# Merging the last two value batches of each head pair in a two-layer transformer kernel

## The chip, the cores and the metric

The kernel runs on one core of a Trainium2 chip. Times are microseconds of device time for one launch. The time before is the median of three runs, 3097.34 us (3094.24 to 3098.24).

## The reference

Eight sequences of 512 tokens with 256 channels pass through two layers. Only the first layer's attention is touched. It has 16 heads and three attentions that share the queries; their outputs are mixed by a gate for each sequence:

```python
a1 = _attn(q, k1, v1, causal=True)    # keys and values from a latent of 32
a2 = _attn(q, ks, vs, causal=False)   # 64 selected tokens only
a3 = _attn(q, kw, vw, causal=True)    # keys and values of their own
g = gate[:, :, None, None, None]
out = g[:, 0] * a1 + g[:, 1] * a2 + g[:, 2] * a3
```

with `_attn` = softmax(q k^T / sqrt(96)) v, values 32 wide. Behind it come the output projection, a feed-forward part, and the second layer (causal attention with rotary positions, 16 heads of 16, and a product with signs).

## The kernel before

The work is cut into passes, one per layer and sequence, in the order (layer, sequence) = (0,0), (0,1), (1,0), (0,2), (1,1), ... (0,7), (1,6), (1,7). "Pass 5" below is layer 0 of sequence 5. A layer-0 pass runs over 8 pairs of heads, 0 to 7.

**Units.** For each pair the transposed scores are made in 12 units, each one psum bank of up to 128 keys by 512 queries: units 0 and 1 are A1's keys 0 to 127 for the two heads, 2 and 3 A1's key blocks 1 and 3, 4 and 5 A3's block 0, 6 and 7 A3's blocks 1 and 3, 8 and 9 block 2 of both A1 and A3 (256 queries each), 10 and 11 A2's 64 selected keys. `unit` (L1162 to L1164) issues three matmuls for each part on TensorE. ScalarE takes the exponential of the bank into one of eight slots of PR (L1839), GpSimd clears what lies above the diagonal (L1954), not for units 10 and 11, which are not masked.

**Batches.** The products with the values are issued by `values` (L1198) in batches listed in PV; batch k holds units 2k and 2k+1. Each part gives two matmuls per head, one with the values and one with a block of ones (row sums), into four column groups of the array (`128*32`, for A2 `64*32`), all accumulated in one psum bank for each attention: OB[A1], OB[A3], OB[A2]. Batch 4 (units 8 and 9) completes A1 and A3, batch 5 (units 10 and 11) A2; COMPLETE says so. A batch ends by raising `pv_done`.

**Behind a batch.** When an attention is complete, ScalarE copies its bank times the gate (`outputs`, L1824) and raises `evacuated`; behind the copy of A2, SP gathers the row sums by DMA (L836), VectorE inverts them (L1454), SP parks and spreads the inverses, VectorE scales the outputs (L1461), GpSimd sums the three (L1970, L1972) and raises `summed`.

**Next operands.** While pair p runs its units, the keys and values of the next pair are made in "pieces" on TensorE: pieces 0 to 3 and 4 (L1066, L1070), the latent keys (L1073), the latent values (L1076), piece 6 for the selected rows (L1081), each followed by transposes (`piece_tr`, L1093). ScalarE copies the results (L1724), VectorE multiplies by the rotary tables (L1400), and subtracts to get the low halves of a high/low split (L1390, L1419). The results of pieces, transposes, units and the row maxima (`max`, L1128) share a ring of five psum banks, taken in the planned order: a step waits until the bank's use five steps back has been read.

**Order.** `attention_steps` gives each step a planned time and sorts by it; every engine runs its steps in that one order. A unit i of pair p stands at 12p + i, a batch at 12p + its last unit + o["pv"], which is 2.66 here, an output at 0.3 behind its batch, the gather at 0.35. So on TensorE the end of a pair looks like this:

```
... unit 10, piece 1, mt, unit 11, pieces 2 and 3, piece_tr 0,
BATCH 4,
unit 0 of the next pair, piece 4, piece_tr 1, unit 1 of the next pair, piece 6, piece_tr 3,
BATCH 5,
unit 2 of the next pair, ...
```

(which pieces stand there varies a little with the pair). In pair 7 there is no next pair. Between its batches stand, in passes 0 to 6, steps that prepare the next pass, above all 16 matmuls that select rows by a one-hot matrix (L1051), made by VectorE (L1590). Behind batch 5 of pair 7 layer 1's work begins: ScalarE copies stacked rows (L1724, PR from R), GpSimd prepares them (L2018, L2020), TensorE transposes them (L1283). In pass 7 nothing stands between the two batches of pair 7.

Of the kernel before, what the change touches and what calls it, by code (L numbers as in the profile page):

```python
# [43 lines left out]
A1, A3, A2 = 0, 1, 2  # L44
# [65 lines left out]
def diagonal(layer, i):  # L110

    return [col for a, _, _, col in UNITS[layer][i] if layer or a != A2]


CAUSAL = [[i for i in range(NU[layer]) if diagonal(layer, i)] for layer in range(2)]
MASK0 = [0, NPAIR * len(CAUSAL[0])]
PV = [(2 * k, 2 * k + 1) for k in range(6)]
NPV = len(PV)


# [10 lines left out]
def before_pass(layer, s):  # L131

    done = [z[0] for z in PASSES[:PASSES.index((layer, s))]]
    return [sum(per[z] for z in done) for per in
            ([NPAIR * n for n in NU], [NPAIR * len(c) for c in CAUSAL], PRODUCTS, OUTS)]


UNIT0, MASK0, PV0, OUT0 = ({z: before_pass(*z)[k] for z in PASSES} for k in range(4))

COMPLETE = {4: [A1, A3], 5: [A2]}  # L140

# [147 lines left out]
def attention_steps(layer, s):  # L291
# [26 lines left out]
    def output(t, what, a, last):  # L318
        at.extend([(t + 0.3, ("out", what, a)), (t + 0.35, ("gather", what))][0:1 + last])
        if last and what < JOBS[layer] - 1:  # L320
            late = "late_" if layer == 0 and what == JOBS[0] - 2 else ""
            t1 = t + 0.35 + o[late + "recip"]
            normalise((layer, s, what), t1, t1 + o[late + "scale"])
# [8 lines left out]
    for p in range(NPAIR):  # L332
        for i in range(0 if layer else n):
            at.append((n * p + i, ("unit", p, i)))
            if i in CAUSAL[layer]:
                at.append((n * p + i + 1.2, ("mask", p, i)))
        for k, units in enumerate(() if layer else PV):
            t = n * p + units[-1] + o["pv"]
            at.append((t, ("pv", p, k)))
            for a in COMPLETE.get(k, []):  # L340
                output(t, p, a, a == A2)
# [203 lines left out]
def build_program(nc, x, w_small, w_imp, w_q, w_nv, w_kw, w_sel, w_proj, g_q, g_kv,  # L545
# [4 lines left out]
    with ctx:  # L550
# [83 lines left out]
        def sem(name):  # L634
            return ctx.enter_context(nc.semaphore(name))
# [4 lines left out]
        pv_done = sem("pv_done")  # L640
# [13 lines left out]
        exp_masked = sem("exp_masked")  # L654
        evacuated = sem("evacuated")
# [90 lines left out]
        def unit_number(s, layer, p, i):  # L746
            if layer:
                return UNIT0[layer, s] + len(QUAD) * (p // 2) + QUAD.index((p % 2, i))
            return UNIT0[layer, s] + p * NU[layer] + i
# [30 lines left out]
        def products_of(j):  # L780
# [5 lines left out]
            p, i = divmod(j - UNIT0[layer, s], NU[layer])  # L786
            return PV0[layer, s] + p * NPV + [i in units for units in PV].index(True) + 1

# [129 lines left out]
        def _(pe):  # L918
# [250 lines left out]
            def values(s, p, k):  # L1169

                units = PV[k]
                if units[-1] in CAUSAL[0]:
                    pe.wait_ge(exp_masked, MASK0[0, s] + p * len(CAUSAL[0]) + CAUSAL[0].index(units[-1]) + 1)
                else:
                    pe.wait_ge(exp_ready, unit_number(s, 0, p, units[-1]) + 1)
                if p and k in (0, 2, 5):

                    pe.wait_ge(evacuated, OUT0[0, s] + 3 * (p - 1) + {0: A1, 2: A3, 5: A2}[k] + 1)  # L1180
                elif s and k == 0:
                    pe.wait_ge(evacuated, OUT0[0, s])
                parts = [(i, part) for i in units for part in UNITS[0][i]]

                parts.sort(key=lambda x: (x[1][0], x[1][2], x[1][1]))
                for n in range(0, len(parts), 2):
                    for side in range(2):
                        for i, (a, h, j, col) in parts[n:n + 2]:
                            rows = KEEP if a == A2 else P
                            if side:  # L1190
                                v = ONES[0:rows, :]
                            elif a == A2:
                                v = VS[:, p % 3, h * VD:(h + 1) * VD]
                            else:
                                v = VV[:, p % 3, j, a, h * VD:(h + 1) * VD]
                            row = 64 * side + 32 * h
                            slot = unit_number(s, 0, p, i) % NP
                            last = mm(OB[a][row:row + 32, j * P:T], v, PR[0:rows, slot, col:col + T - j * P],  # L1198
                                      start=(j == 0), stop=(j == 2 or a == A2), skip_group_check=True)
                last.then_inc(pv_done, 1)  # L1200
# [85 lines left out]
            def attention(layer, s):  # L1286
                for x in STEPS[layer, s]:
# [6 lines left out]
                    elif x[0] == "max":  # L1294
                        max_scores(s, layer, x[1], x[2])
                    elif x[0] == "mt":
                        transpose_maxima(s, layer, x[1])
                    elif x[0] == "unit":
                        unit(s, layer, x[1], x[2])
                    elif x[0] == "pv" and layer == 0:  # L1300
                        values(s, x[1], x[2])
                    elif x[0] == "pv":
                        values_of_heads(s, x[1], x[2])
                    elif x[0] == "pro_pe":
                        prologue(x[1], x[2])
                    elif x[0] in ("wo_early", "wo_last", "sign") or x[0] == "hT" and x[2] == 3:
                        tail(x)
                    elif x[0] == "proj_early":
                        project_early(x[1])
                    elif x[0] == "proj_last":  # L1310
                        project_last(x[1])
                    elif x[0] == "hT":
                        transpose_half(x[1], x[2], x[3])
                    elif x[0] == "fc":
                        hidden_units(*x[1:])
                    elif x[0] == "y":
                        second_products(*x[1:])
                    elif x[0] == "qk":
                        queries_and_keys(*x[1:])
                    elif x[0] == "v":  # L1320
                        values_of_half(*x[1:])
                    elif x[0] == "heads":
                        transpose_heads(*x[1:])
# [396 lines left out]
        def _(act):  # L1720
            a = nc.scalar

            def copy(dst, src):
                return a.activation(dst, src, ACT.Copy)  # L1724
# [89 lines left out]
            def outputs(s, layer, n, att):  # L1814

                if layer == 0:
                    act.wait_ge(pv_done, PV0[0, s] + n * NPV + (6 if att == A2 else 5))
                    if s + n:
                        act.wait_ge(summed, NPAIR * s + n)
                    if n == 0:  # L1820
                        act.wait_ge(gates_ready, s + 1)
                        act.wait_ge(scaled1, NG * max(s - 1, 0))
                    g = 1 if att == A1 else 2 if att == A3 else 0
                    a.activation(OE[:, att, :], OB[att][:, :], ACT.Copy, scale=GG[:, g:g + 1]).then_inc(evacuated, 1)  # L1824
                else:
                    act.wait_ge(pv_done, PV0[1, s] + (n + 1) * len(QUAD_PV))
                    if n == 0:
                        act.wait_ge(summed, NPAIR * min(s + 2, B))
                    if s and n < 3 or n >= 3:
                        act.wait_ge(scaled1, NG * s + max(n - 2, 0))  # L1830
                    copy(OE[:, n % 3, :], OB[n % 3][:, :]).then_inc(evacuated, 1)
# [280 lines left out]
```

## Time and profile before

| | |
|---|---|
| median of the runs | 3097.34 us |
| the profiled execution | 3094.82 us |
| its span | 3093.1 us |
| TensorE busy | 2884.6 us (93%) |
| VectorE busy | 1980.4 us (64%) |
| ScalarE busy | 1483.6 us (48%) |
| GpSimd busy | 958.1 us (31%) |
| matmuls at L1198 | 2304 with ones, 2048 with VV, 256 with VS |
| mean granted TensorE clock | 0.968 |

The span runs from the first to the last instruction of one profiled execution; 1.7 us of its own time lie outside. PE is TensorE, PEld its weight loads, DVE VectorE, ACT ScalarE, POOL GpSimd. Matmuls are pipelined and their ends are modelled, so the distances between the starts of matmuls are read rather than their durations. The granted clock is the share of full speed.

### The profile page before, as it was taken

The numbers are of one execution on the slowest core, as the hardware profiler recorded it, in microseconds if no ns is written. First come the engines' busy times: TensorE is split into PE (matmuls) and PEld (weight loads), VectorE is DVE, ScalarE is ACT, GpSimd is POOL, SyncE is SP. The second block draws the span as 40 slices with busy tenths as digits, with TensorE's granted clock in tenths as the row PEclk, the third lists the DMA queues.
The fourth block names the chain that finished last, engine by engine and source line by source line (L and its number), as shares of the span: only waits on it lengthen the run. The fifth ranks groups of instructions, "written<-read, shape, count | busy, mean of one in ns | idle before, by whom it ended". The sixth has DMA issues, their size and how long they took to land. (4 is left out here: it accounts for less than half of the span.)

```text
span 3093.1 us, 53525 instructions
## 1 busy us (share of the span) xinstructions
PE 2884.6 (93%) x18384; PEld 2056.4 (66%) x18384; DVE 1980.4 (64%) x6275; ACT 1483.6 (48%) x3132; POOL 958.1 (31%) x1700
## 2 busy tenths in 40 slices
PE   6999899989999899999999989998999989999877
PEld 5666676667766677666776667666676666766654
DVE  5666557675586656766666766677566676665644
ACT  2554344464445644455445554445544554445433
POOL 1233232432333313333233332233223332333231
PEclk8999999999999999999999999999999999999989
DMA  3111001001110010100111001110011000110000
GB/s 121 33 33 31 27 26 37 19 18 33 35 33 19 24 37 26 32 24 19 37 32 33 17 26 37 33 31 14 27 39 32 26 18 23 32 32 18 14 8 29
DMA packets 58700, 91.42 MB, mean 30 GB/s; under 512 B 19904, under 2 KB 32704, under 8 KB 58176
## 3 DMA queue, kind: packets, MB, share of 16 engines
q1 hardware_dynamic: 58432, 88.01, 9.6%
q8 instruction: 148, 2.42, 0.3%
q14 instruction: 120, 0.98, 0.1%
HBM read 81.68 MB, written 5.24 MB: 28 GB/s over the span
## 5 line engine op out<-in xcount | busy, mean ns | idle before, releaser
L1839 ACT ACTIVATE PR<-work 128x512 f32<-128x512 f32 (+1 forms) x1088 | 640.3, 598 | 715.6 <-PE work L1164 608.9
L1438 DVE CUSTOM_DVE_ANT_0 work<-work,KEEPB 128x128 f32<-128x128 f32 (+3 forms) x1536 | 665.8, 477 | 95.6 <-PE work L1128 94.1
L1954 POOL TENSOR_SCALAR_AFFINE_SELECT PR<-PR 128x256 f32<-128x256 f32 (+1 forms) x960 | 362.0, 381 | 872.7 <-ACT PR L1839 868.4
L1128 PE MATMUL work<-BIG 96*128 96x448 f32 (+8 forms) x1664 | 454.6, 364 | 31.8 <-DVE NMX L1438 17.4
L1162 PE MATMUL work<-BIG 99*128 99x512 f32 (+4 forms) x1152 | 420.0, 365 | 11.0 <-DVE BIG L1419 8.6
L1943 POOL TENSOR_TENSOR TOK<-AB 128x256 f32<-128x256 f32 (+1 forms) x320 | 216.6, 677 | 636.7 <-DVE AB L1400 601.6
L1198 PE MATMUL outs<-PR,ONES 128*32 128x512 f32 (+4 forms) x2304 | 407.7, 461 | 0.0
L1419 DVE TENSOR_TENSOR BIG<-work,BIG 96x512 fp32r<-96x512 f32 (+1 forms) x320 | 191.5, 604 | 324.3 <-ACT BIG L1724 324.0
L1128 PEld LDWEIGHTS work<-BIG 96*128 96x128 f32 (+1 forms) x1664 | 278.5, 199 | 157.6 <-issue 64.1
L1163 PE MATMUL work<-BIG 96*128 96x512 f32 (+4 forms) x1152 | 382.7, 332 | 0.0
L1164 PE MATMUL work<-BIG 96*128 96x512 f32 (+4 forms) x1152 | 380.6, 330 | 0.0
L1724 ACT ACTIVATE BIG<-work 96x512 fp32r<-96x512 f32 (+5 forms) x624 | 353.4, 569 | 40.0 <-PE work L1093 29.4
L1198 PE MATMUL outs<-PR,VV 128*32 128x512 f32 (+3 forms) x2048 | 337.7, 440 | 3.7 <-POOL PR L1954 3.7
L1724 ACT ACTIVATE TOK<-work 128x128 f32<-128x128 f32 (+1 forms) x320 | 85.5, 267 | 516.8 <-issue 229.3
L1162 PEld LDWEIGHTS work<-BIG 99*128 99x128 f32 (+1 forms) x1152 | 210.1, 182 | 167.1 <-issue 100.7
L1070 PE MATMUL work<-WKW,HT 128*128 128x256 f32 x1024 | 276.5, 394 | 0.0
L1400 DVE TENSOR_TENSOR AB<-work,ROPE 128x512 f32<-128x512 f32 (+1 forms) x320 | 201.0, 629 | 114.7 <-PE work L1070 91.0
L1441 DVE TENSOR_REDUCE NMX<-work 128x1 f32<-128x64 f32 (+1 forms) x640 | 170.4, 283 | 123.4 <-PE work L1128 119.6
L1164 PEld LDWEIGHTS work<-BIG 96*128 96x128 f32 (+1 forms) x1152 | 213.1, 185 | 23.8
L1163 PEld LDWEIGHTS work<-BIG 96*128 96x128 f32 (+1 forms) x1152 | 212.6, 185 | 8.3 <-issue 2.0
L1070 PEld LDWEIGHTS work<-WKW,HT 128*128 128x128 f32 x1024 | 196.0, 198 | 16.2
L1093 PE MATMUL work<-ID,TOK 128*96 128x128 f32 x1152 | 179.5, 275 | 18.3 <-ACT VV L1724 4.2
(178 smaller groups left out, 4620.1 us busy)
## 6 DMA issues: line engine op xcount, KB each, us to landing
NRM<-park SPq DMA_DIRECT2D x112, 192.0 KB, 3.1
WKW<-w_kw_dram SPq DMA_DIRECT2D x64, 256.0 KB, 2.7
WSEL<-w_sel_dram SPq DMA_DIRECT2D x64, 256.0 KB, 3.0
R<-park SPq DMA_DIRECT2D x72, 64.0 KB, 2.0
HN<-x_dram SPq DMA_DIRECT2D x8, 512.0 KB, 4.8
X<-x_dram SPq DMA_DIRECT2D x8, 512.0 KB, 3.9
out_dram<-X SPq DMA_DIRECT2D x7, 512.0 KB, 3.2
R<-park SPq DMA_DIRECT2D x16, 192.0 KB, 3.0
```

Source lines behind the costliest of these rows:

```text
L1070: last = mm(ps[:, 192:448], HT0[:, c, t * P:(t + 1) * P], WKW[:, g % 2, c, :], start=(c == 0), stop=(c == NC - 1))
L1128: last = mm(ps[:, col:col + n], q, k, start=(i_mm == 0), stop=(i_mm == len(u["mm"]) - 1))
L1162: mm(out, k[0][0:D0 + 3], q[0][0:D0 + 3], start=(col == 0), stop=False)
L1163: mm(out, k[0][0:D0], q[1][0:D0], start=False, stop=False)
L1164: last = mm(out, k[1][0:D0], q[0][0:D0], start=False, stop=stop)
L1198: last = mm(OB[a][row:row + 32, j * P:T], v, PR[0:rows, slot, col:col + T - j * P], start=(j == 0), stop=(j == 2 or a == A2), skip_group_c ...
L1400: read_work(v.tensor_tensor(rotations(i, rows, heads), src.unsqueeze(1).broadcast_to(shape), ROPE0[0:rows, t, :, :].unsqueeze(2).broadcast ...
L1438: last = v.tensor_tensor_reduce(ps[:, lo:hi], ps[:, lo:hi], KEEPB[:, T - (hi - lo):T], -1.0, -NEG, ALU.add, ALU.min, dst)
L1724: return a.activation(dst, src, ACT.Copy)
L1839: a.activation(PR[0:rows, j % NP, :], ps[0:rows, :], ACT.Exp).then_inc(exp_ready, 1)
L1943: gp.tensor_tensor(dst.rearrange("p h (j d) -> p h j d", j=2), a4, b4[:, :, ::-1, :], ALU.add).then_inc(tok_ready, 1)
L1954: gp.affine_select(blocks, blocks, [[0, len(cols)], [1, P]], ALU.is_ge, 0.0, base=0, channel_multiplier=-1).then_inc(exp_masked, 1)
```

## The change

PV gets five batches instead of six: the last holds units 8, 9, 10 and 11 and completes A1, A3 and A2. By the planning rule its time is 12p + 11 + 2.66, which is where batch 5 stood. Before it, TensorE waits for the mask of unit 9, the exponential of unit 11, and for the previous pair's A2 output to be copied (A1's and A3's were awaited by batches 0 and 2). The copies of A1 and A3 are planned at 0.3 behind the merged batch, ahead of A2's, and wait for the fifth `pv_done` of the pair. The matmuls themselves, and their order within a batch (A1, A3, A2), are the same.

```diff
-PV = [(2 * k, 2 * k + 1) for k in range(6)]
+PV = [(2 * k, 2 * k + 1) for k in range(4)] + [(8, 9, 10, 11)]
...
-COMPLETE = {4: [A1, A3], 5: [A2]}
+COMPLETE = {4: [A1, A3, A2]}
...
                 units = PV[k]
-                if units[-1] in CAUSAL[0]:
-                    pe.wait_ge(exp_masked, MASK0[0, s] + p * len(CAUSAL[0]) + CAUSAL[0].index(units[-1]) + 1)
-                else:
+                masked = [i for i in units if i in CAUSAL[0]][-1]
+                pe.wait_ge(exp_masked, MASK0[0, s] + p * len(CAUSAL[0]) + CAUSAL[0].index(masked) + 1)
+                if masked != units[-1]:
                     pe.wait_ge(exp_ready, unit_number(s, 0, p, units[-1]) + 1)
-                if p and k in (0, 2, 5):
+                if p and k in (0, 2, 4):
 
-                    pe.wait_ge(evacuated, OUT0[0, s] + 3 * (p - 1) + {0: A1, 2: A3, 5: A2}[k] + 1)
+                    pe.wait_ge(evacuated, OUT0[0, s] + 3 * (p - 1) + {0: A1, 2: A3, 4: A2}[k] + 1)
...
-                    act.wait_ge(pv_done, PV0[0, s] + n * NPV + (6 if att == A2 else 5))
+                    act.wait_ge(pv_done, PV0[0, s] + n * NPV + 5)
```

## Rows read from the trace of the kernel before

**Rows 1.** The page's first part: busy time, share of the span, instructions.

```profile
PE 2884.6 (93%) x18384; PEld 2056.4 (66%) x18384; DVE 1980.4 (64%) x6275; ACT 1483.6 (48%) x3132; POOL 958.1 (31%) x1700
```

**Rows 2.** Waits of TensorE: us in total, times, longest us.

```profile
PE work L1283 <- POOL PR L2020: 17.7, 15, 8.2
...
PE work L1081 <- DVE BIG L1419: 5.8, 18, 0.7
...
PE work L1066 <- DVE BIG L1390: 3.0, 8, 0.9
```

**Rows 3.** Timeline of TensorE, pass 5, pair 5 to 6: start, duration, [wait].

```profile
2059.59 0.60 PE L1093 MATMUL work<-ID,TOK 128*96 128x128 f32 x4
...
2061.12 0.50 PE L1162 MATMUL work<-BIG 99*128 99x512 f32 x1
...
2063.59 0.50 PE L1162 MATMUL work<-BIG 99*128 99x512 f32 x1
...
2064.86 1.13 PE L1081 MATMUL work<-WSEL,SELT 128*128 128x256 f32 x4 [0.29 <-DVE BIG L1419]
...
2066.36 0.62 PE L1198 MATMUL outs<-PR,VS 64*32 64x512 f32 x2
```

**Rows 4.** Timeline of TensorE, pass 4: transposes, then a unit, no batch between.

```profile
1552.60 0.60 PE L1093 MATMUL work<-ID,TOK 128*96 128x128 f32 x4
1552.95 0.48 PE L1162 MATMUL work<-BIG 99*128 99x512 f32 x1
```

**Rows 5.** Timeline of TensorE, end of pass 7: starts of batches 4 and 5.

```profile
2853.38 0.41 PE L1198 MATMUL outs<-PR,VV 128*32 128x256 f32 x2
...
2854.38 0.62 PE L1198 MATMUL outs<-PR,VS 64*32 64x512 f32 x2
```

**Rows 6.** Timeline of ScalarE in the stretch of rows 3.

```profile
2059.64 1.20 ACT L1724 ACTIVATE BIG<-work 32x512 fp32r<-32x512 f32 x2
2063.14 0.28 ACT L1724 ACTIVATE TOK<-work 128x128 f32<-128x128 f32 x1 [2.31 <-issue]
...
2063.90 1.26 ACT L1824 ACTIVATE NRM<-outs,GG 128x512 f32<-128x512 f32 x2
...
2068.31 0.68 ACT L1824 ACTIVATE NRM<-outs,GG 128x512 f32<-128x512 f32 x1
```

**Rows 7.** Timeline of VectorE in the stretch of rows 3.

```profile
2060.94 1.40 DVE L1390 TENSOR_TENSOR BIG<-work,BIG 32x512 fp32r<-32x512 f32 x2 [3.63 <-ACT BIG L1724]
2062.37 0.69 DVE L1400 TENSOR_TENSOR AB<-work,ROPE 128x512 f32<-128x512 f32 x1
2064.12 0.69 DVE L1419 TENSOR_TENSOR BIG<-work,BIG 96x512 fp32r<-96x512 f32 x1 [1.06 <-ACT BIG L1724]
```

**Rows 8.** Timelines of VectorE and TensorE, pass 5, pair 1 to 2.

```profile
1926.79 0.69 DVE L1419 TENSOR_TENSOR BIG<-work,BIG 96x512 fp32r<-96x512 f32 x1 [1.06 <-ACT BIG L1724]
...
1928.02 0.48 PE L1162 MATMUL work<-BIG 99*128 99x512 f32 x1
```

**Rows 9.** Timeline of VectorE, pass 3, behind pair 1's outputs.

```profile
1184.27 0.55 DVE L1454 RECIPROCAL NRM<-NRM 48x64 f32<-48x64 f32 x1 [0.26 <-DMA NRM<-NRM]
```

**Rows 10.** Timelines of TensorE, ScalarE and GpSimd, end of pass 5.

```profile
2112.61 0.62 PE L1198 MATMUL outs<-PR,VS 64*32 64x512 f32 x2
...
2114.14 0.69 ACT L1824 ACTIVATE NRM<-outs,GG 128x512 f32<-128x512 f32 x1 [0.22 <-PE outs L1198]
2114.85 1.15 ACT L1724 ACTIVATE PR<-R 128x512 fp32r<-128x512 f32 x2
...
2116.08 0.73 POOL L2018 TENSOR_TENSOR PR<-R,PR 128x256 fp32r<-128x256 f32 x1 [1.32 <-ACT PR L1724]
...
2117.56 1.20 PE L1283 MATMUL work<-ID,PR 128*128 128x128 f32 x9 [0.37 <-POOL PR L2020]
```

**Rows 11.** Windows: us, busy (x) of PE, PEld, DVE, ACT, POOL, granted clock, DMA, GB/s.

```profile
1813.00:1820.00 7.00, 4.61 (x27) 3.13 (x28) 6.00 (x13) 5.93 (x12) 1.29 (x4) 1.00 0.04 10
...
2113.12:2116.50 3.38, 3.38 (x20) 2.48 (x13) 0.47 (x1) 3.13 (x7) 1.84 (x6) 0.50 0.01 2
```

## The prediction

> **What bounds the kernel now.** I read the page first. TensorE is busy 2884.6 of 3093.1 us (93%), VectorE 64%, ScalarE 48% [rows 1]: TensorE sets the pace, so the terms to count are instructions that leave TensorE and stretches in which it is made to wait. The second view was the table of waits of TensorE. Two of its lines lie where the change works: TensorE waits 18 times in front of L1081 (the products with the selected rows' weights, piece 6 of a pair) for VectorE's low parts of L1419, and 8 times in front of L1066 (piece 4) for L1390; at the pass ends it waits for GpSimd's L2020 in front of the transposes of L1283 [rows 2]. The sums are small (5.8 and 3.0 us), but they say that at 26 places TensorE already arrives before its operand or its bank is there. Third, the timelines of the stretch between the old batch of units 8 and 9 (batch 4) and that of units 10 and 11 (batch 5).
>
> **What the change does to TensorE's own work.** The same 72 matmuls of L1198 run per pair. Batch 4 (16 matmuls over 256 columns) leaves its place ahead of unit 0 of the next pair and runs right in front of batch 5, behind unit 0, piece 4, the transposes of piece 1, unit 1, piece 6 and the transposes of piece 3. In its old place, from the transposes before it to the unit after it, TensorE takes 2061.12 - 2059.59 = 1.53 us [rows 3]; the same succession without a batch between takes 1552.95 - 1552.60 = 0.35 [rows 4]. So it costs 1.18 us there. In pass 7 the two batches already stand next to each other, and batch 5 starts 2854.38 - 2853.38 = 1.00 us after batch 4 [rows 5]. So if TensorE never waited, each of the 56 boundaries between two pairs of a pass (8 passes of 7) would gain 1.18 - 1.00 = 0.18 us.
>
> The Trainium skill, "TensorEngine Tiling (Array Packing)", section "Key Properties", says that changing the tiling mode drains TensorE. That agrees with the 0.18 us: the merged batch still has two modes (128*32, then 64*32), so one change of four goes. By that rule alone the sum would be -10 us; it is the first rival below.
>
> **What is late next.** Batch 4 is also what TensorE does while others prepare its next operands. In pair 5 of pass 5: ScalarE copies the key parts until about 2060.84 [rows 6]; that releases VectorE's L1390 (2060.94, 1.40 us), then L1400 (2062.37, 0.69) [rows 7], then ScalarE's copy at 2063.14 [rows 6], which frees the psum bank that unit 1 takes at 2063.59 [rows 3]. The following copy releases L1419 at 2064.12, which ends at 2064.81 [rows 7]; piece 6 starts at 2064.86, after 0.29 us of waiting [rows 3]. Nothing in this chain depends on batch 4: its first link is a product that TensorE makes ahead of it. With batch 4 gone TensorE reaches unit 1 some 1.2 us sooner, finds no bank, and starts unit 1 and piece 6 when it did before. The 1.00 us of the batch is then added in front of batch 5. So a boundary with spare time s (from the last operand's arrival to the step's start, the smallest in the stretch) costs 1.18 - s - 0.18, and where s is over 1.18 it gains 0.18.
>
> - 26 boundaries [rows 2] have s of 0.04 (2064.86 less 2064.81, one semaphore's way): 26 x 0.96 = 25.0 us.
> - 23 have s near 0.54, as pair 1 of pass 5, where the low part ends at 1926.79 + 0.69 = 1927.48 and unit 1 starts at 1928.02 [rows 8]: 23 x 0.46 = 10.6.
> - 7 (nearly all of them pair 0 of a pass) have more than 1.18: 7 x -0.18 = -1.3.
>
> I sorted the 56 by following these chains in the timelines. Sum: +34.3. Its ends: if only the 26 lose, and the others gain, +19.6; if all but the seven lose in full, +45.7.
>
> **ScalarE's outputs.** The copies of A1 and A3 out of their banks (L1824, two in 1.26 us) move from 2063.90 to behind the merged batch, next to A2's (0.68) [rows 6]. Two take 1.26 us and one 0.68, so they follow each other 0.57 apart, and ScalarE ends three in a row 1.14 us later than one, beside the 1.0 us of TensorE. Queued behind them are exponentials and copies that free banks. Bounds: from -0.1 per boundary (the exponential of unit 0, now behind the two copies, comes 1.2 us sooner) to +1.14 where a bank behind is waited for. ScalarE is busy 48% of the time; I take 0, and keep +20 us (some 18 boundaries in full) for the range. The gather of the row sums on the DMA queue of SP, which waits for A2's copy, and VectorE's reciprocals behind it move with it. In pair 1 of pass 3 the reciprocal already waits 0.26 us for that gather [rows 9], and behind it on VectorE stand the maxima of the next pair; it may come 1.14 us late beside TensorE there, 8 us over the pairs of that number, which the same 20 us hold.
>
> **The pass ends.** For pair 7 batch 4 moves behind L1051, which ends as late as now, because it waits for VectorE's one-hot rows. In pass 5 batch 5 starts at 2112.61 [rows 10]; now both run from there. TensorE's clock is granted at half speed from 2113.12 to 2116.50 [rows 11], so the added 1.00 us at full speed becomes about 2.0 (0.5 before the fall, the rest and batch 5 at half). The last output starts at 2114.14 now [rows 10]; in the new order three start after about 2116.1, the last ends some 2.0 + 1.14 = 3.1 us later than now. Behind it on ScalarE stands the copy of the next stack (2114.85 now), then GpSimd's L2018 and L2020, then the transposes of L1283, which already wait for GpSimd (2117.56, 0.37 us of waiting) [rows 10]: there is no cover. Between 2.0 (TensorE's delay alone) and 3.1 (ScalarE's) I take 2.6: six passes, 15.6 us; pass 7 2.0 (two more outputs, and the merged batch waits for the last exponential), pass 0 0.5. Sum +18.1; ends 8 and 26.
>
> **Sum.** 34.3 + 0 + 18.1 = 52.4. On the profiled execution (3094.82, of which 1.7 us lie outside the span) that is 3147 us; the median of the runs is 2.5 us above the profiled one. Forecast 3147; with the ends of the terms 3125 to 3170.
>
> **Rivals.**
> - *Only the saved change of mode counts (faster).* TensorE would reach unit 1 early and find its bank, because the bank comes from a chain that starts earlier too. It decides from the point where s exceeds 1.18 us at most boundaries: 56 x 0.18 = 10 us, 3085. For it: the seven boundaries; against it: the 26 waits of rows 2 and the absence of batch 4 from the chain. 0.07.
> - *Given back later.* TensorE comes 1 us later to the units behind, and waits that it now has there (VectorE's maxima, masks) shrink; 7% of the span is idle TensorE [rows 1]. Half of the 34 returned, or the pass ends absorbed by layer 1: 3094.8 + 17 to 34 is 3112 to 3129; I count what lies under 3125 here. Against: most idle time lies at the pass ends. 0.14.
> - *No change.* Gains at idle chains cancel losses: within 6 us. Nothing in the rows asks for it. 0.05.
> - *Worse than summed.* The three outputs hold up banks (+20), or the longer waits let the clock fall. Half speed is seen at such a pass end, over 3.4 us [rows 11], costing up to 1.7 us; at all 26 waiting boundaries that were +44, 3191. Against: in a stretch of 7 us in which TensorE was busy for only 4.61 the granted clock stayed at 1.00 [rows 11], and the new waits would be 1.2 to 1.5 us. 0.12 for over 3170. (The Trainium skill, "TensorE: Matmul & The Clock Gate", section "What's actually happening", has the throttled state as the default, released by activity; the half-speed stretch behind the pass end's wait agrees, and no row shows a fall inside a pair loop.)
>
> **How the numbers follow.** Main case 0.62 (3125 to 3170), rivals 0.07, 0.14, 0.05, 0.12. The range 3106 to 3172 leaves out faster, no change, and the ends of the last: about 0.2. 0.2% (6 us) is what a measurement can tell from no change: faster 0.08, same 0.06, slower 0.86.
>
> **What would show it.** In the profile after, pair 5 of pass 5: TensorE idle for about 1.2 us ahead of L1162 or L1081, with the waits of L1081, L1066 and L1162 on VectorE and ScalarE grown by some 30 us together; pair periods 1 us longer in pairs 2, 3, 5 and unchanged in pair 0; at the pass ends L1283 2 to 3 us later against L1051. It is wrong if TensorE's idle time in these stretches does not grow (first rival), if the boundary loses but the pair period does not (second), or if the granted clock falls within a pass.

## The result: 3172.0 us, slower by 2.4%

Four runs of the changed kernel gave 3172.02 us (3168.70 to 3174.68), the kernel before 3096.82 (3094.24 to 3098.24): a ratio of 1.0243, 95% interval 1.0226 to 1.0261. The forecast was 3147, and its range ended at 3172, where the median now lies: the sign was right, the loss was 75 us instead of 52.

The page of the changed kernel, first the busy times, then the line of its core with the mean granted clock:

```profile
span 3172.9 us, 53533 instructions
PE 2914.0 (92%) x18384; PEld 2072.2 (65%) x18384; DVE 1979.6 (62%) x6275; ACT 1479.4 (47%) x3132; POOL 960.7 (30%) x1700
```

```profile
core 0: 3172.9 us, clock 0.960
```

Against [rows 1], the instructions of TensorE are as many as before, but it is busy 29 us longer. More work can't be the reason; the same work ran slower. The mean granted clock is 0.960 against 0.968, which at two levels, 1 and 0.5, is 2 x 0.040 x 3172.9 = 254 us at half speed against 198. (The mean has three digits, so such a sum is good to some 3 us.)

The waits of TensorE (us in total, times, longest):

```profile
PE work L1283 <- POOL PR L2020: 24.3, 17, 8.6
...
PE work L1051 <- DVE AB L1590: 17.7, 7, 3.5
PE work L1162 <- DVE BIG L1419: 12.1, 22, 0.6
PE work L1066 <- DVE BIG L1390: 11.9, 8, 1.5
PE work L1093 <- DVE BIG L1390: 11.3, 26, 0.7
...
PE work L1162 <- ACT VV L1724: 8.9, 18, 0.6
...
PE work L1081 <- DVE BIG L1419: 6.1, 19, 0.7
PE work L1162 <- ACT BIG L1724: 6.0, 8, 0.8
```

Those of the kernel before that [rows 2] does not have:

```profile
PE work L1051 <- DVE AB L1590: 10.4, 7, 3.0
...
PE work L1093 <- DVE BIG L1390: 3.5, 8, 0.5
...
PE work L1162 <- ACT VV L1724: 0.2, 1, 0.2
```

The wait that [rows 2] showed in front of L1081 has hardly grown (5.8 to 6.1). The new idle time stands one or two steps ahead of it: L1066 from 3.0 to 11.9, L1162 behind ScalarE's VV from 0.2 to 8.9, L1093 behind L1390 from 3.5 to 11.3. The timeline of TensorE at the boundary of [rows 3], pass 5, pair 5 to 6, shows why:

```profile
2119.86 0.60 PE L1093 MATMUL work<-ID,TOK 128*96 128x128 f32 x4
2120.22 0.48 PE L1162 MATMUL work<-BIG 99*128 99x512 f32 x1
...
2122.75 0.61 PE L1093 MATMUL work<-ID,TOK 128*96 128x128 f32 x4 [0.40 <-DVE BIG L1390]
2123.86 0.50 PE L1162 MATMUL work<-BIG 99*128 99x512 f32 x1 [0.49 <-ACT VV L1724]
...
2125.13 1.13 PE L1081 MATMUL work<-WSEL,SELT 128*128 128x256 f32 x4 [0.30 <-DVE BIG L1419]
...
2126.62 0.41 PE L1198 MATMUL outs<-PR,VV 128*32 128x256 f32 x2
...
2127.62 0.62 PE L1198 MATMUL outs<-PR,VS 64*32 64x512 f32 x2
```

TensorE now waits 0.40 + 0.49 + 0.30 = 1.19 us where it waited 0.29, and reaches piece 6 (L1081) 2125.13 - 2119.86 = 5.27 us behind the transposes, as before (2064.86 - 2059.59). The merged batch is then added: the first product with A2's values starts 7.76 us behind the transposes instead of 6.77. The loss up to there is 0.99 us; the forecast had 0.96.

What the forecast had left out of its sum is seen at another boundary, pass 6, pair 3 to 4, first in the timeline of TensorE and then in windows (us, busy times of PE, PEld, DVE, ACT, POOL, granted clock, DMA share, GB/s):

```profile
2439.52 0.61 PE L1093 MATMUL work<-ID,TOK 128*96 128x128 f32 x4 [0.46 <-DVE BIG L1390]
2440.62 0.50 PE L1162 MATMUL work<-BIG 99*128 99x512 f32 x1 [0.49 <-ACT VV L1724]
...
2441.89 1.65 PE L1081 MATMUL work<-WSEL,SELT 128*128 128x256 f32 x4 [0.29 <-DVE BIG L1419]
2443.33 1.06 PE L1093 MATMUL work<-ID,TOK 128*96 128x128 f32 x4
2444.32 0.64 PE L1198 MATMUL outs<-PR,VV 128*32 128x256 f32 x2
```

```profile
2437.00:2442.40 5.40, 4.16 (x20) 2.83 (x19) 3.42 (x7) 2.20 (x6) 0.73 (x1) 1.00 0.29 97
2442.41:2445.80 3.39, 3.39 (x23) 1.74 (x21) 2.12 (x7) 1.42 (x5) 1.65 (x3) 0.50 0.35 88
2445.90:2450.00 4.10, 4.10 (x38) 2.63 (x34) 1.98 (x7) 3.50 (x9) 1.01 (x3) 1.00 0.12 46
```

Behind the three waits the clock is granted at half speed for 3.4 us. This boundary costs 2.45 us. The same boundary in pass 5 costs 0.84: its three waits are as long (0.45, 0.49 and 0.30 us), but the clock stays up (a window around them):

```profile
2053.00:2060.00 7.00, 5.76 (x42) 3.49 (x44) 4.46 (x11) 2.57 (x9) 2.34 (x4) 1.00 0.29 84
```

Of the 18 boundaries with these three waits 6 have a fall, one each in passes 0, 2, 3, 4, 6 and 7. The 6 boundaries of pair 2 in passes 2 to 7, with two longer waits (1.50 us ahead of L1066, 0.56 ahead of unit 1), have none. A seventh fall, in pass 1, stands inside pair 4, away from the boundary, and there is one in that pair too in the kernel below that changes only the pass ends, where it costs nothing. In the profile before there is none between the first batches of pairs 0 and 7. Which of the waits bring the clock down, and which do not, is not explained.

The end of pass 5, first the one-hot products in the kernel before (timeline of TensorE), then the changed kernel (TensorE, ScalarE, a window):

```profile
2110.71 1.97 PE L1051 MATMUL work<-AB,HN 128*128 128x64 f32 x16 [1.56 <-DVE AB L1590]
```

```profile
2172.37 3.34 PE L1051 MATMUL work<-AB,HN 128*128 128x64 f32 x16 [2.49 <-DVE AB L1590]
2175.65 0.64 PE L1198 MATMUL outs<-PR,VV 128*32 128x256 f32 x2
...
2179.38 3.67 PE L1283 MATMUL work<-ID,PR 128*128 128x128 f32 x16
2183.94 1.97 PE L1283 MATMUL work<-ID,PR 128*128 128x128 f32 x16 [0.89 <-POOL PR L2020]
```

```profile
2179.51 1.84 ACT L1824 ACTIVATE NRM<-outs,GG 128x512 f32<-128x512 f32 x3 [7.96 <-PE outs L1198]
```

```profile
2172.70:2182.80 10.10, 10.10 (x55) 6.90 (x54) 1.82 (x4) 3.29 (x6) 3.55 (x7) 0.50 0.01 2
```

Batch 4 no longer fills the time ahead of L1051, so TensorE waits 2.49 us there instead of 1.56, and half speed now begins with L1051 and lasts 10.1 us, where it began behind it and lasted 3.4 [rows 11]. The 16 matmuls of L1051 take 2175.65 - 2172.37 = 3.28 us instead of 1.90 (2112.61 of [rows 10] less 2110.71), so the merged batch starts 1.38 us later than the forecast put it. In passes 1 to 6 their starts are spread over 2.9 to 3.2 us instead of 1.7. The transposes of L1283 that wait for GpSimd come 2183.94 - 2172.37 = 11.57 us behind L1051's start instead of 6.85 (2117.56 of [rows 10] less 2110.71): 4.72 us later, where the forecast had 2 to 3.

### The profile page after: what moved, and what is told of

Same layout as the page of the kernel before. It is cut to its first block and busy times, and to the rows that moved or that the text cites. A ratio compares the mean times of both kernels' runs of the same rounds, so it can differ in the third digit from the quotient of the medians.

```text
span 3172.9 us, 53533 instructions
## 1 busy us (share of the span) xinstructions
PE 2914.0 (92%) x18384; PEld 2072.2 (65%) x18384; DVE 1979.6 (62%) x6275; ACT 1479.4 (47%) x3132; POOL 960.7 (30%) x1700
## 5 line engine op out<-in xcount | busy, mean ns | idle before, releaser
L1128 PE MATMUL work<-BIG 96*128 96x448 f32 (+8 forms) x1664 | 455.7, 365 | 33.0 <-DVE NMX L1438 18.8
L1162 PE MATMUL work<-BIG 99*128 99x512 f32 (+4 forms) x1152 | 422.4, 367 | 28.3 <-DVE BIG L1419 12.1
L1419 DVE TENSOR_TENSOR BIG<-work,BIG 96x512 fp32r<-96x512 f32 (+1 forms) x320 | 191.7, 605 | 383.8 <-ACT BIG L1724 383.3
L1198 PE MATMUL outs<-PR,ONES 128*32 128x512 f32 (+4 forms) x2304 | 415.8, 472 | 0.0
L1164 PE MATMUL work<-BIG 96*128 96x512 f32 (+4 forms) x1152 | 381.1, 331 | 0.0
L1198 PE MATMUL outs<-PR,VV 128*32 128x512 f32 (+3 forms) x2048 | 347.1, 451 | 3.9 <-POOL PR L1954 3.1
L1162 PEld LDWEIGHTS work<-BIG 99*128 99x128 f32 (+1 forms) x1152 | 210.8, 183 | 170.7 <-issue 78.2
L1164 PEld LDWEIGHTS work<-BIG 96*128 96x128 f32 (+1 forms) x1152 | 213.6, 185 | 23.7
L1093 PE MATMUL work<-ID,TOK 128*96 128x128 f32 x1152 | 182.2, 278 | 26.1 <-DVE BIG L1390 11.3
```

The source lines that it names most:

```text
L1128: last = mm(ps[:, col:col + n], q, k, start=(i_mm == 0), stop=(i_mm == len(u["mm"]) - 1))
L1162: mm(out, k[0][0:D0 + 3], q[0][0:D0 + 3], start=(col == 0), stop=False)
L1164: last = mm(out, k[1][0:D0], q[0][0:D0], start=False, stop=stop)
```

## The experiments

The kernel before ran beside every group: 3094.4 to 3095.3 us. Times are medians; where pair boundaries or pass ends are given, they are differences in the profiled executions, from the first batch of one pair to the first batch of the next, summed (boundaries), and from the first batch of pair 7 to the next layer-0 pass, in pass 7 to the end of the span (ends).

**Fillers in the new waits.** The changed kernel, and in the place where batch 4 stood the same 16 matmuls once more, into A2's bank, where nobody reads them: at the 26 boundaries of the forecast that wait in full, and at the ends of passes 0 to 6.

```diff
+        if layer == 0 and (p == NPAIR - 1 and s < B - 1 or p in ([0, 1, 2, 3, 4, 5] if s == 0 else [1, 4] if s == 1 else [2, 3, 5])):
+            at.append((n * p + 9 + o["pv"], ("fill", p)))
...
+    mm(OB[A2][row:row + 32, j * P:T], v, PR[0:P, slot, col:col + T - j * P], start=True, stop=True, ...)
```

> Five batches as in the change; in addition TensorE repeats the 16 matmuls of units 8 and 9 in the place where batch 4 stood, into A2's bank, where nobody reads them (the merged batch overwrites them): at the 26 pair boundaries where TensorE waits in full, and at the ends of passes 0 to 6. Theory (the forecast's waits are right, and what it missed is the clock: the profile after has 258 us at half speed against 197): the filler runs inside the waits and adds no time, the half-speed time goes back to about 200 us, and the kernel gets FASTER than the changed one by about half of the 61 us less what was waiting anyway: 3145 to 3152 us. Rival (the missing 23 us are ScalarE's three outputs in a row): the filler changes nothing or costs its switches of mode, 3172 to 3180.

3151.91 us (3149.32 to 3153.70), inside the expected range and 20 us faster than the changed kernel, with 528 matmuls more. The mean granted clock is 0.969: 2 x 0.031 x 3150.0 = 195 us at half speed, as before the change. The boundary of pass 6, pair 3 in this kernel, timeline and windows (L1217 is the filler, L1164, L1083 and L1200 are the L1162, L1081 and L1198 of the other kernels):

```profile
2417.30 0.41 PE L1217 MATMUL outs<-PR,VV 128*32 128x256 f32 x2
...
2420.82 0.50 PE L1164 MATMUL work<-BIG 99*128 99x512 f32 x1
...
2422.09 1.13 PE L1083 MATMUL work<-WSEL,SELT 128*128 128x256 f32 x4 [0.29 <-DVE BIG L1439]
...
2423.59 0.41 PE L1200 MATMUL outs<-PR,VV 128*32 128x256 f32 x2
```

```profile
2416.25:2421.65 5.40, 5.40 (x40) 3.66 (x38) 3.39 (x6) 3.04 (x7) 0.73 (x1) 1.00 0.28 97
2421.66:2425.05 3.39, 3.10 (x30) 1.72 (x32) 2.27 (x8) 1.25 (x5) 1.66 (x3) 1.00 0.24 43
```

The three waits are one of 0.29 again, the clock stays at 1.00, and the boundary costs 0.83 us instead of 2.45. The filler itself costs nothing here: it runs where TensorE waited.

**Fillers at the boundaries only.** The first condition without the pass ends.

> The same filler, only at the 26 pair boundaries, not at the pass ends. Theory: the seven or eight falls of the clock inside the passes go (about 30 us at half speed, some 13 us of time), those at the pass ends stay: about 3159 us. Rival (outputs): 3172 to 3178.

3159.14 us (3157.15 to 3162.97), the time as expected. The boundaries come to +41.5 us (49.6 in the changed kernel, 39.7 with both fillers), the pass ends stay at +25.8 (29.1, and 15.2 with both). By the medians 13 of the 20 us come with the fillers at the boundaries and 7 with those at the ends; by the profiles it is 8 (49.6 less 41.5) and 11 (25.8 less 15.2), so the split is rough. Within the pairs only the fall of pass 1 is left, but the half-speed time did not go down by the expected 30 us: this profiled execution, the slowest of its four, has 2 x 0.040 x 3161.2 = 253 us of it, as much as the changed kernel, more of it between pair 7 and the next layer-0 pass.

**The move without the merge.**

```diff
             t = n * p + units[-1] + o["pv"]
+            if k == 4:
+                t += 1.99
             at.append((t, ("pv", p, k)))
```

> The kernel before with its six batches and their own signals; only batch 4 is planned directly ahead of batch 5, in its new place. Theory: the place does all of it, so the time is that of the changed kernel, 3166 to 3175 us, a little under it where A1's and A3's copies start 0.65 us sooner than behind the merged batch. Rival (the merge itself costs: one wait for four units, three outputs released at once): well under it, 3140 us or less.

3156.69 us (3152.15 to 3159.57): below the expectation, above the rival's. The place makes 62 of the 77 us of that comparison, and the merge 15. In its profile, that of the fastest of its four executions, three falls of the clock stand within the pairs, not seven, the ends are +18.8 instead of +29.1, and some boundaries without a fall cost 0.05 to 0.24 us less (pair 2 in pass 5 0.87 against 0.98, pair 5 in pass 6 1.34 against 1.59). Why the same move lets the clock fall less often when the two batches have signals of their own is not settled.

**The two halves of the move.** The same edit with `k == 4 and p < NPAIR - 1` and with `k == 4 and p == NPAIR - 1`.

> Six batches; batch 4 planned directly ahead of batch 5 in pairs 0 to 6 only, the pass ends as before. In the profile of the kernel with batch 4 moved everywhere the loops between the pairs take 38 us more and the pass ends 19. Theory (the two add): 3095 + 38 = 3130 to 3136 us. Rival (the loops' delay is recovered at the undisturbed pass ends): 3120 or less.

> The same move in pair 7 only, at the pass ends. Theory (the two add): 3095 + 19 = 3110 to 3117 us, with more half-speed time than before at each pass end. Rival (layer 1 absorbs it): 3100 or less.

3134.38 us (+39) and 3114.92 (+20): they add to +59 beside +62 for both. Neither is recovered by the other.

**Half the way.** `if k == 4 and p < NPAIR - 1: t += 1.29`, which puts batch 4 behind piece 4 and the transposes, ahead of unit 1 and piece 6.

> Six batches; in pairs 0 to 6 batch 4 moves only half the way, behind unit 0, piece 4 and the transposes of piece 1 of the next pair, but still ahead of unit 1 and piece 6. Theory (it matters which waiting step the batch is moved past): only the boundaries whose wait is in front of piece 4 (8 of them) lose the 0.96 us; the 18 that wait at unit 1 or piece 6, and the 23 with 0.54 us spare there, keep their cover: 3095 + 8, so 3100 to 3107 us. Rival (the loss goes by the distance): half of 38, 3112 to 3117.

3106.54 us (3102.94 to 3112.80), +11, in the expected range and under the rival's: by the steps moved past, not by the distance. That the sum fits is in part luck. In passes 2 to 7 pair 2, whose wait is in front of piece 4, cost only 0.21 us, because it waits a second time in front of unit 1, where the batch now found its place; pair 6, which I had left out, cost 0.68 in passes 2 to 6, and two boundaries with a fall of the clock in passes 0 and 1 make 4.8 of the profile's 14.4 us at the boundaries.

**Early.** The changed kernel with the merged batch where batch 4 stood (`if k == 4: t -= 2.0`).

> Five batches as in the change, but the merged batch is planned two units sooner, where batch 4 stood (its copies, gather and normalising as much sooner). Theory: TensorE keeps work where the next operands are late, now 1 us more of it, one change of mode less per pair (56 x 0.18 = 10 us), the 0.3 us waits at the 26 boundaries covered (8 us), less idle ahead of the one-hot products: 3070 to 3090 us, faster than both. Rival (the merge itself costs, wherever it stands, since its last exponential comes late): 3100 us or more.

3195.78 us (3189.66 to 3202.79): slower than both, a clear miss. Step by step against the kernel before, the boundaries with pieces behind them gain (unit 2 of the next pair starts 0.2 us sooner in pass 5, pair 4), but before that, within the pair, the row maxima of pair 4 come 0.65 to 2.65 us late. The inverses and scalings, planned two units earlier too, stand among these maxima on VectorE; that they are the cause is argued, and the next kernel tests it only together with the copies. And in pair 6, where fewer pieces stand behind unit 11, the batch waits 1.4 us for unit 11's exponential, and a batch of pair 7 2.0 us for its mask.

**Early, products alone.** The kernel before, with batch 5 behind batch 4 on TensorE, nothing else moved.

```diff
-            at.append((t, ("pv", p, k)))
+            at.append((t - 1.99 if k == 5 and p < 6 else t, ("pv", p, k)))
```

> The six batches and the plan of before, but in pairs 0 to 5 TensorE runs batch 5 directly behind batch 4, two units sooner; copies, gather and normalising stay at their planned times. In the early merged kernel the boundaries themselves gained 0.2 to 0.7 us each, and what it lost came behind them, at steps that wait for the normalising work moved with the batch, and in pair 6 at unit 11's exponential. Theory: without these two the gain stays: 48 boundaries by 0.2 to 0.5 us, 3072 to 3086 us, faster than both. Rival (it is the products themselves that are too early, their loss shows later in the pair): 3095 or more.

> As the kernel in which batch 5 runs directly behind batch 4 in pairs 0 to 5, but only in pairs 0, 1, 2 and 4, whose boundaries gained 0.2, 0.2, 1.0 and 0.2 us in its profile, and not in pairs 3 and 5 (0.0 and a loss of 0.47). Theory: about 1.6 us in each of passes 2 to 7, some 12 in all: 3081 to 3087 us. Rival (what is gained sets off falls of the clock or waits elsewhere, as in that kernel, which gained 5 us for a forecast of 15): 3088 to 3095.

3090.25 us, a ratio of 0.9984 to the kernel before (0.9971 to 0.9996), and with pairs 0, 1, 2 and 4 alone 3089.46, 0.9984 (0.9975 to 0.9993). Both are faster than the kernel before, by 5 us where some 15 and 12 were expected: the first lies between theory and rival, the second in the rival's range. The boundaries gain what they should (0.2, 0.2 and 1.0 us in pairs 0, 1 and 2), but 0.4 to 0.7 us come back in pair 5, and a fall of the clock or two takes the rest.

**Three copies in a row, alone.** All batches in their old places, the copies of A1 and A3 next to A2's.

```diff
-                output(t, p, a, a == A2)
+                output(t + 1.99 * (k == 4), p, a, a == A2)
```

> The kernel before with all six batches where they stood; only ScalarE's copies of A1 and A3 are planned next to A2's, so that it makes three in a row as in the changed kernel, with TensorE's work and order untouched. In the changed kernel the batch of units 2 and 3 behind pair 5's outputs started 0.57 us late for its mask, and the moved batch without the merge was 15 us faster than the changed kernel. Theory (three copies in a row hold up a few exponentials, the rest of the 15 us is clock): 0.2 to 0.6 us at one or two pair boundaries of each pass, some 3 to 8 us in all, 3098 to 3104. Rival A (ScalarE has room for them): 3095, no change. Rival B (the copies are the whole 15 us): 3108 or more.

3118.06 us (3107.50 to 3120.78), +23, rival B. This was a surprise: ScalarE is busy 48% of the time, yet the copies cost as much as everything at the pass ends. In pass 5 behind pair 4, its timelines of ScalarE, VectorE and GpSimd:

```profile
2054.38 1.82 ACT L1824 ACTIVATE NRM<-outs,GG 128x512 f32<-128x512 f32 x3
2056.09 0.59 ACT L1839 ACTIVATE PR<-work 128x512 f32<-128x512 f32 x1
2056.57 0.59 ACT L1724 ACTIVATE BIG<-work 96x512 fp32r<-96x512 f32 x1
```

```profile
2057.26 0.69 DVE L1419 TENSOR_TENSOR BIG<-work,BIG 96x512 fp32r<-96x512 f32 x1 [1.99 <-ACT BIG L1724]
...
2060.75 0.68 DVE L1376 TENSOR_TENSOR HN<-work,SIN 128x512 f32<-128x512 f32 x1
```

```profile
2061.52 1.27 POOL L2002 TENSOR_TENSOR R<-HN 128x512 f32<-128x512 f32 x1 [4.36 <-DVE HN L1376]
```

The key copy behind the three is late, so VectorE's L1419 is (it waits 1.99 us; 0.97 at that place before), and everything that stands behind it in VectorE's order, among it a step of the other layer, L1376. GpSimd waits for that with L2002, and the masks of the units stand behind L2002 in its order. The batch of units 2 and 3 came 1.03 us late, 4.35 us behind the batch ahead of it instead of 3.32. In passes 2 to 6 pair 5 costs 1.13 to 1.36 us. The changed kernel has the same chain at the same place, with less left of it, presumably since TensorE itself is late by then (0.50 us of waiting instead of 0.94):

```profile
2098.91 0.69 DVE L1419 TENSOR_TENSOR BIG<-work,BIG 96x512 fp32r<-96x512 f32 x1 [2.04 <-ACT BIG L1724]
...
2103.17 1.29 POOL L2002 TENSOR_TENSOR R<-HN 128x512 f32<-128x512 f32 x1 [4.35 <-DVE HN L1376]
...
2104.87 0.52 PE L1198 MATMUL outs<-PR,VV 128*32 128x384 f32 x2 [0.50 <-POOL PR L1954]
```

## Why the prediction was right in its mechanism and short in its size

**The bound and what is late next: right.** TensorE lost time where it was moved past steps that wait for VectorE and ScalarE, and not where there was cover. In passes 2 to 7 the boundaries without a fall moved by (medians) -0.13 us (pair 0; forecast -0.18), +0.56 (pair 1; +0.46), +0.97 (pair 2; +0.96), +0.84 (pair 3; +0.96), +0.33 (pair 4; +0.46; it gave back 0.35 or more behind a fall in pair 3) and +0.48 (pair 6; +0.46). At the clock of the kernel before, which the fillers restore, the 56 boundaries come to +39.7 us, one fall of the clock in pass 1 still among them; the forecast had +34.3. In one link the reading was off: the copy that frees unit 1's bank is not ScalarE's at 2063.14 but the next, of VV (2063.32, 0.22 us), which L1162 waits for in the changed kernel; the place of the wait is the same.

**ScalarE's outputs at 0: wrong, and a small part of the miss.** Pair 5 cost 1.57 us instead of 0.96, through the chain above. In passes 2 to 6, where it did so with fillers throughout, that is 3 us. The step named "exponentials and copies that free banks" as what is queued behind; it was a key copy, and the wait ran over three engines in their fixed orders. Its own price is 23 us (the experiment), of which TensorE's delay seems to hide most in the changed kernel; that is argued from the shorter wait. The bound kept for it, +20, was about right.

**The pass ends at +18.1: about right at the old clock, wrong at the one granted.** With both fillers, whose half-speed time is in sum that of the kernel before, they come to +15.2; in the changed kernel to +29.1 (+2.9 in pass 0, forecast +0.5; +4.0 to +4.9 in passes 1 to 6, forecast +2.6; -0.5 in pass 7, forecast +2.0). The first step that failed is "which ends as late as now" of L1051. It starts as late as before, 13.4 us behind the first batch of pair 7 in pass 5 (13.5 before), but it runs at half speed, because the wait ahead of it grew by the batch that no longer fills it. With the fillers its starts are spread over 1.7 us again in passes 0 to 4 (2.4 and 1.9 in passes 5 and 6). I had moved the batch into a half-speed stretch and taken the stretch itself from the kernel before. The sum with the fillers hides a spread, from 0.0 in pass 1 to +5.0 in pass 5, where half speed lasts 13.7 us.

**The clock: the term that carried the miss.** The second step that failed is that a fall of the clock inside a pass was put at nothing in the sum. It was a rival at "all 26 waiting boundaries" for +44 us or none, with 0.12 for over 3170, and "if the granted clock falls within a pass" was the prediction's own sign of being wrong. What came was a fall at 6 of the 26, some 1.6 us each, and longer stretches at the ends: 59 us more at half speed than with fillers (254 against 195), and 20 us of time. The row against it (a stretch of 7 us in which TensorE was busy for only 4.61 without a fall) was one case, and did not exclude it. 52 of the forecast and 20 of the clock make 72 of the measured 75. That the 52 fit so well at the old clock is in part luck: the boundaries were 5 us over it and the ends 3 under.

**The range.** The ends of the three terms add up to 3117 (19.6 - 5.6 + 8 over 3094.8) and 3187 (45.7 + 20 + 26), not to 3125 and 3170; the prediction does not say how it got from the one to the other. The measured time lies inside the wider pair.

**Rivals.** "Only the saved change of mode" falls: the waits are there, and TensorE's busy time rose. "Given back later" falls: the halves add, and nothing is recovered behind the boundary. A saving of its size is seen: where there is cover, the early products gain 0.2 us a boundary.

The Trainium skill, "TensorE: Matmul & The Clock Gate", section "What's actually happening", has the clock set by how busy TensorE has been of late. The fillers agree: 528 useless matmuls, put into waits, took the mean granted clock from 0.960 to 0.969 and made the kernel 20 us faster.

## What to carry to other kernels

A piece of work in a fixed order is also cover for whatever is being prepared beside it: before merging or moving it, list the waits of the steps that it would be moved past, since each one that is already there turns the move into a loss of the whole piece. Where the engine that loses its cover is TensorE, price the waits twice, once as time and once as clock: half speed came behind waits of 0.46, 0.49 and 0.29 us close together, at 6 of 18 boundaries that had about these three, so the clock's price is an average and not a rule. And an engine that is busy half of the time can still have no room for three copies in a row, if other engines' orders hang on the instruction behind them.

## What the runs showed of the hardware

The spread between runs of one kernel follows the granted clock: in ten runs of the kernel with early products in pairs 0 to 5 the slowest (3098.5 us) had a mean clock of 0.963 and the fastest (3081.3) 0.972, so 57 us less at half speed for 17 us of time. A difference of 5 us between two kernels is thus within what the falls of one execution make, and only the medians of ten runs could tell it.
